# Early fusion block with routed experts: the shared expert of five pairs stands in its own turn instead of in a block behind the main loop

## What is computed

```python
def _L0_ffn_ref(x, gate_w, w1, w3, w2, sw1, sw3, sw2):
    xf = x.reshape(-1, d)
    scores = jax.nn.sigmoid(xf @ gate_w.T)
    top_scores, top_idx = jax.lax.top_k(scores, K)
    ...
    h = jax.nn.silu(einsum('ecd,edh->ech', buf, w1)) * einsum('ecd,edh->ech', buf, w3)
    y = jnp.einsum('ech,ehd->ecd', h, w2)
    ...
    shared = jax.nn.silu(xf @ sw1) * (xf @ sw3) @ sw2
    return (shared + routed).reshape(bs, slen, d)
...
h = jnp.concatenate([tokens(x), txt], axis=1)
h = h + attn(layernorm(h))
h = h + ffn(layernorm(h))
```

## Time and profile before

| | us |
|---|---|
| runs of the kernel before | 1791.42, 1799.02, 1825.51 |
| median | 1799.02 |
| span of the profiled execution | 1823.6 |
| the one run that can hold that span | 1825.51 |
| PE busy (share of the span) | 1534.0 (84%) |
| DVE busy | 1421.6 (78%) |
| ACT busy | 1256.5 (69%) |
| POOL busy | 1226.0 (67%) |

### The profile page before, as it was taken

The page is one execution under the profiler, slowest core; times in us unless marked ns, Lnnn a source line. Parts: engine busy times, 40 slices in busy tenths (PEclk is TensorE's granted clock), DMA queues, the critical chain, the costliest instruction groups (busy, mean ns, idle before and its releaser), DMA issues.

```text
span 1823.6 us, 30829 instructions
## 1 busy us (share of the span) xinstructions
PE 1534.0 (84%) x9237; PEld 1158.6 (64%) x9237; DVE 1421.6 (78%) x5705; ACT 1256.5 (69%) x2195; POOL 1226.0 (67%) x973
## 2 busy tenths in 40 slices
PE   2888998999899999888989898999889975676672
PEld 1566776777676767656767666677667764554552
DVE  3477997999797988777888888889888975587661
ACT  2897997988788878777878787889878851111110
POOL 1025776777676767666667676777667767488887
PEclk9899999999999999999999999999999998899886
DMA  9965666666666666556555655566656221476653
GB/s 182 229 138 120 138 139 125 123 121 124 102 117 100 117 101 106 96 103 103 95 101 104 108 102 102 101 111 105 103 103 103 63 59 40 96 116 109 98 88 35
DMA packets 267117, 197.21 MB, mean 108 GB/s; under 512 B 65464, under 2 KB 246437, under 8 KB 266953
## 3 DMA queue, kind: packets, MB, share of 16 engines
q1 hardware_dynamic: 210120, 174.84, 50.2%
q0 software_dynamic: 51200, 17.87, 8.4%
q10 hardware_dynamic: 5633, 2.56, 0.7%
HBM read 86.24 MB, written 85.39 MB: 94 GB/s over the span
## 4 chain that ended last, share of the span: by engine, by line
PE 40%; ACT 22%; issue 11%; POOL 9%; another core or an unknown queue 8%; DVE 7%; DMA 3%; SPq 0%; ACTq 0%; POOLq 0%; DVEq 0%
POOL out_rows L639 6%; PE bank L919 5%; PE bank L999 5%; ACT img L656 5%; ACT xh L739 4%; PE bank L1087 3%; PE bank L982 3%; POOL slot_rows L605 3%; PE bank L946 2%; PE bank L1018 2%; PE bank L1078 2%; ACT xs L726 2%; ACT kq L793 2%; ACT kq L792 2%
## 5 line engine op out<-in xcount | busy, mean ns | idle before, releaser
L605 POOL DMA_INDIRECT slot_rows<-xs,slot x768 | 874.1, 1138 | 284.5 <-issue 247.3
L656 ACT ACTIVATE img<-img 84x980 f32<-84x980 f32 x190 | 339.6, 1788 | 14.8 <-DMA img<-in_x 7.2
L591 POOL TENSOR_TENSOR rs<-ve,neg_half 128x12 f32<-128x12 f32 (+1 forms) x66 | 150.3, 2277 | 234.4 <-DVE ve L1342 232.8
L919 PE MATMUL bank<-img,w_tok 126*128 126x392 f32 (+1 forms) x640 | 228.7, 505 | 27.9 <-DMA img<-img 23.3
L639 POOL DMA_INDIRECT out_rows<-img,etok x128 | 198.7, 1552 | 64.0 <-issue 35.0
L919 PEld LDWEIGHTS bank<-img,w_tok 126*128 126x128 f32 (+1 forms) x640 | 124.0, 195 | 113.3 <-issue 23.3
L982 PEld LDWEIGHTS bank<-pos_a,v 128*128 128x128 f32 x768 | 145.4, 198 | 54.0 <-issue 10.8
L982 PE MATMUL bank<-pos_a,v 128*128 128x325 f32 (+2 forms) x768 | 163.8, 351 | 6.1 <-issue 3.8
L726 ACT ACTIVATE xs<-h,nb,rs 128x128 f32<-128x128 f32 x384 | 154.0, 481 | 3.0 <-DVE nb L1348 3.0
L739 ACT ACTIVATE xh<-h,nb,rs 128x128 f32<-128x128 f32 x384 | 154.0, 480 | 1.3 <-DVE nb L1348 1.3
L1499 DVE TENSOR_TENSOR h<-bank,hbo 128x768 f32<-128x768 f32 x64 | 61.1, 955 | 114.6 <-remote 103.3
(11 more groups left out here) (217 smaller groups left out, 3697.1 us busy)
## 6 DMA issues: line engine op xcount, KB each, us to landing
img<-in_x SPq DMA_DIRECT2D x384, 150.1 KB
img<-img SPq DMA_DIRECT2D x254, 160.8 KB
img<-img SPq DMA_DIRECT2D x128, 128.6 KB
out_rows<-fin SPq DMA_DIRECT2D x128, 128.0 KB
slot_rows<-xs,slot POOLq DMA_INDIRECT x768
slot_rows<-init_rows SPq DMA_DIRECT2D x16, 540.0 KB, 9.1
img<-slot_rows SPq DMA_DIRECT2D x32, 270.0 KB
h<-in_txt SPq DMA_DIRECT2D x64, 128.0 KB
```

The lines of the kernel that those rows point to most:

```text
L591: g.tensor_tensor(out=rs[:, q.u, half:], in0=ve[:, q.u, half:], in1=neg_half[:, half:], op=ALU.pow).then_inc(S["p_rs"], 1)
L605: g.indirect_dma_start(out=slots_d, out_offset=bass.IndirectOffsetOnAxis(ap=slot[0:nt, q.x, r, part:part + 1], axis=0), in_=xs[0:nt, q.x, ...
L656: a.activation(cols[:, b0:b0 + nb, :], raw[:, q.u, :].rearrange("p (t b) -> p b t", b=P)[:, b0:b0 + nb, :], ACT.Copy)\
L919: ins = mm(bank[:, 5, 0:2 * PATCHES], w_tok[r, m, :], xk[r, k.u, :, m, :], start=(m == 0), stop=(m == SHIFT - 1))
```

## The change

Every pair's shared expert is computed in its own turn. `LATER`, `later`, `rows_of`, `columns_of`, `load_later`, `store_later`, `later_hidden`, `later_out`, `later_product` and `later_sum` go, with their calls, eight semaphores and the buffers `x2_l` and `rows_l`. PE's, POOL's and DVE's waits for the block's semaphores go too. The core of the diff:

```diff
-LATER = tuple(range(8, PAIRS, 11))[0:5]
...
-        x2_l = sb("x2_l", [D, len(LATER), 2, L])
-        rows_l = sb("rows_l", [128, len(LATER) - 1, 2 * NT, D])
...
-            def load_later():
-
-                sp.wait_ge(s_init, 16 * (SLOTS // 1024 + 1))
-                for i, c in enumerate(LATER):
-                    sp.wait_ge(s_store[c % 2], (c // 2 + 1) * 16 * NT)
...
-                    for x, (t0, _) in enumerate(TILES):
-                        sp.dma_start(f[:, x], o[t0:t0 + TILE]).then_inc(l_rows, 16)
...
-                if k.c == PAIRS - 1:
-                    load_later()
...
-            pool.wait_ge(l_store, 16 * NT * len(LATER))
...
-                a.activation(columns_of(z)[:, :, :], bank[:, 1:3, 0:L], ACT.Copy).then_inc(S["a_x2t"], 1)
+                a.activation(x2_t[:, :, :], bank[:, 1:3, 0:L], ACT.Copy).then_inc(S["a_x2t"], 1)
...
-                if later(z):
-                    a.activation(sl[:, 0, 0:TILE], bank[:, 0, 0:TILE], ACT.Silu).then_inc(S["a_sl"], 1)
-                else:
-                    a.activation(sl[:, :, :], bank[:, 0:2, 0:L], ACT.Silu).then_inc(S["a_sl"], 1)
+                a.activation(sl[:, :, :], bank[:, 0:2, 0:L], ACT.Silu).then_inc(S["a_sl"], 1)
...
-            for i in range(len(LATER)):
-                act.wait_ge(l_f1, i + 1)
-                if i == 0:
-                    act.wait_ge(S["v_fin"], PAIRS)
-                else:
-                    act.wait_ge(l_su, i)
-                a.activation(sl[:, :, :], bank[:, 1:3, 0:L], ACT.Silu).then_inc(l_sl, 1)
-                if i > 1:
-                    store_later(i - 2)
...
-                if later(w):
-                    tr(bank[:, 4, 0:TILE], ident, ident).then_inc(S["pe_o"], 1)
-                    return
...
-                if later(z):
-                    tr(bank[:, 4, 0:TILE], ident, ident).then_inc(S["pe_f3b"], 1)
-                else:
-                    mm(bank[:, 4, 0:L], sw3[:, :], x2_t[:, 1, :], start=True, stop=True).then_inc(S["pe_f3b"], 1)
+                mm(bank[:, 4, 0:L], sw3[:, :], x2_t[:, 1, :], start=True, stop=True).then_inc(S["pe_f3b"], 1)
...
-                if not later(z):
-                    mm(bank[:, 1, 0:L], sw1[:, :], x2_t[:, 1, :], start=True, stop=True)
+                mm(bank[:, 1, 0:L], sw1[:, :], x2_t[:, 1, :], start=True, stop=True)
...
-            def later_hidden(i):
...
-                for s in range(2):
-                    ins = mm(bank[:, 1 + s, 0:L], sw1[:, :], x2_l[:, i, s, :], start=True, stop=True)
-                ins.then_inc(l_f1, 1)
-                if i:
-                    pe.wait_ge(l_su, i)
-                for s in range(2):
-                    ins = mm(bank[:, 3 + s, 0:L], sw3[:, :], x2_l[:, i, s, :], start=True, stop=True)
-                ins.then_inc(l_f3, 1)
...
-            def later_out(i):
...
-            later_hidden(0)
-            for i in range(1, len(LATER)):
-                later_hidden(i)
-                later_out(i - 1)
-            later_out(len(LATER) - 1)
-            pe.wait_ge(l_fin, len(LATER))
...
-                if later(w):
-                    vv.tensor_copy(fin[:, w.u], h2[:, w.u]).then_inc(S["v_fin"], 1)
-                    return
...
-                if not later(z):
-                    TT(su[:, :, :], sl[:, :, :], bank[:, 3:5, 0:L], ALU.mult)
+                TT(su[:, :, :], sl[:, :, :], bank[:, 3:5, 0:L], ALU.mult)
...
-            later_product(0)
-            dve.wait_ge(l_rows, 16 * NT * len(LATER))
-            for i in range(1, len(LATER)):
-                later_product(i)
-                later_sum(i - 1)
-            later_sum(len(LATER) - 1)
```

More of the change, by code:

```diff
@@ L132, in uses @@
         return self.c // of + 1
-LATER = tuple(range(8, PAIRS, 11))[0:5]
-def later(pair):
-    return pair.c in LATER
 def first(pair):
@@ L1024, in shared_3b @@
                 wait(pe, S["a_g"], z, -2)
-                if later(z):
-                    tr(bank[:, 4, 0:TILE], ident, ident).then_inc(S["pe_f3b"], 1)
-                else:
-                    mm(bank[:, 4, 0:L], sw3[:, :], x2_t[:, 1, :], start=True, stop=True).then_inc(S["pe_f3b"], 1)
+                mm(bank[:, 4, 0:L], sw3[:, :], x2_t[:, 1, :], start=True, stop=True).then_inc(S["pe_f3b"], 1)
             def shared_1a(z):
-                if later(z):
-                    tr(bank[:, 0, 0:TILE], ident, ident).then_inc(S["pe_f1a"], 1)
-                else:
-                    mm(bank[:, 0, 0:L], sw1[:, :], x2_t[:, 0, :], start=True, stop=True).then_inc(S["pe_f1a"], 1)
+                mm(bank[:, 0, 0:L], sw1[:, :], x2_t[:, 0, :], start=True, stop=True).then_inc(S["pe_f1a"], 1)
             def logits(z):
@@ L1040, in logits @@
                 for s in range(2):
-                    ins = mm(bank[E * s:E * s + E, 2, 0:L], gate_t[:, :], columns_of(z)[:, s, :], start=True, stop=True)
+                    ins = mm(bank[E * s:E * s + E, 2, 0:L], gate_t[:, :], x2_t[:, s, :], start=True, stop=True)
                 ins.then_inc(S["pe_lgt"], 1)
@@ L1046, in shared_1b @@
                 wait(pe, S["v_h2"], z, -1)
[L1047 to L1048 removed]
+                mm(bank[:, 1, 0:L], sw1[:, :], x2_t[:, 1, :], start=True, stop=True)
             def shared_3a(z):
[L1052 to L1053 removed]
+                mm(bank[:, 3, 0:L], sw3[:, :], x2_t[:, 0, :], start=True, stop=True)
             def transpose_1(k):
@@ L1140, in _ @@
             steps(body, 0, 4)
-            def later_hidden(i):
-                if i == 0:
-                    pe.wait_ge(S["a_lgt"], PAIRS)
-                    pe.wait_ge(S["v_fin"], PAIRS)
-                else:
-                    pe.wait_ge(l_sl, i)
-                for s in range(2):
-                    ins = mm(bank[:, 1 + s, 0:L], sw1[:, :], x2_l[:, i, s, :], start=True, stop=True)
-                ins.then_inc(l_f1, 1)
-                if i:
-                    pe.wait_ge(l_su, i)
-                for s in range(2):
-                    ins = mm(bank[:, 3 + s, 0:L], sw3[:, :], x2_l[:, i, s, :], start=True, stop=True)
-                ins.then_inc(l_f3, 1)
-            def later_out(i):
-                pe.wait_ge(l_su, i + 1)
-                if i == 0:
-                    pe.wait_ge(S["a_lg"], PAIRS)
-                else:
-                    pe.wait_ge(l_fin, i)
-                for s in range(2):
-                    for x, (t0, _) in enumerate(TILES):
-                        ins = mm(bank[:, 6 + s, x * D:(x + 1) * D], su[:, s, t0:t0 + TILE], sw2[:, :], start=True, stop=True)
-                ins.then_inc(l_o, 1)
-            later_hidden(0)
-            for i in range(1, len(LATER)):
-                later_hidden(i)
-                later_out(i - 1)
-            later_out(len(LATER) - 1)
-            pe.wait_ge(l_fin, len(LATER))
             def turn(q):
@@ L1618, in _ @@
             steps(body, 0, 4)
-            def later_product(i):
-                dve.wait_ge(l_f3, i + 1)
-                dve.wait_ge(l_sl, i + 1)
-                if i == 0:
-                    dve.wait_ge(S["pe_o"], PAIRS)
-                else:
-                    dve.wait_ge(l_o, i)
-                TT(su[:, :, :], sl[:, :, :], bank[:, 3:5, 0:L], ALU.mult).then_inc(l_su, 1)
-            def later_sum(i):
-                dve.wait_ge(l_o, i + 1)
-                r = rows_of(i).rearrange("p (s t) d -> p s (t d)", s=2)
-                TT(r, bank[:, 6:8, 0:NT * D], r, ALU.add).then_inc(l_fin, 1)
-            later_product(0)
-            dve.wait_ge(l_rows, 16 * NT * len(LATER))
-            for i in range(1, len(LATER)):
-                later_product(i)
-                later_sum(i - 1)
-            later_sum(len(LATER) - 1)
             def prepare(q):
```

14 lines of the change are left out of this document (removed).

## The result

The changed kernel takes 1744.27 us (median of 4 runs, 1739.89 to 1745.25), the kernel before 1799.74 us beside it (4 runs, 1791.42 to 1825.51): ratio 0.9707, 95% interval 0.9658 to 0.9755. That is faster by 2.9%, where the prediction said 1802 us, a range of 1779 to 1825 and "same" with 0.89. The time, the range and the direction are wrong. The profiled execution of the changed kernel took 1743.62 us with a span of 1741.8 us; the one of the kernel before took 1825.51 us, the longest of its four and 26 us over their median.

The account below looks back on a forecast made before the run. The loop was taken as bound by PE, DVE close behind, plus 2.7 us stall a turn, the experts by POOL. The median 1799.0 + 3 for full turns, 0 for the block and the rest, gave 1802 us, range 1779 to 1825.

Parts of the forecast that it names:

- Term 1: Main loop: computing the five light turns in full adds 0.6 us each, +3 us, with ends -2.5 and +13.1.
- case C: Main loop: PE bounds every quick turn, so each filled turn pays PE's full 2.62 us: +13.1, 1812; chance 0.15.
- Rival D: Main loop: late signals depend on where packets break in a turn; 1763 or less, or 1835 or more; chance 0.13.
- Term 2: Behind the loop: in the profiled execution the block held up the experts; removal gives -7.4 us, ends -9.6 and 0.
- what is late next: Behind the loop: without the block PE idles some 28 us and starts at its lower clock; up to 2.2 us return.
- Term 3: Behind the loop: in a usual execution the block lies wholly beside POOL's scatters, so its removal gives 0.
- Case B: Behind the loop: the block is on the path in the usual run too: 1795 us; chance 0.27.
- Term 4: Loads and stores around the loop's end, POOL's wait, eight semaphores, SBUF of two tensors: cost and gain 0.

Follow-up runs that it names:

- f1: Exact copy of the kernel before, on a chip with signals in time: 1664.66 us, ratio 1.0001 to the kernel before.
- c4: The changed kernel with the five light turns back and no block, leaving out five pairs' shared expert: 1662.96 us, ratio 1.0003 to the kernel before.
- d4: The kernel before with all turns full and the block kept, its sums added times zero, on a late-signal chip: 1765.09 us, ratio 0.9835.
- e1: The kernel before with 128 fulfilled waits ahead of PE's first transposes: 1829.42 us, ratio 0.9890; its sibling with 64 waits: 1823.13 us, 0.9882.
- e3: The kernel before with 33 fulfilled waits on PE in each of the five light turns: 1829.26 us, ratio 0.9919.
- e4: The kernel before with all turns full and the block kept, its sums added times zero: 1811.67 us, ratio 0.9811.
- f4: The changed kernel with 128 fulfilled waits ahead of PE's first transposes: 1669.48 us, ratio 1.0031 to the kernel before.
- c1: The changed kernel itself on another chip, signals in time: 1668.33 us against 1663.08 for the kernel before, ratio 1.0032.
- f2: The changed kernel with five light turns and no block, leaving out five pairs' shared expert: 1662.76 us, ratio 0.9989 to the kernel before.
- g2: The changed kernel with five light turns and no block, leaving out five pairs' shared expert, run once more: 1662.81 us, ratio 0.9996 to the kernel before.
- d1: The changed kernel again, on a late-signal chip: 1751.67 us against 1791.23 for the kernel before, ratio 0.9759.
- c2: The changed kernel with the block's two buffers allocated but unused: 1669.16 us, ratio 1.0036 to the kernel before.
- c3: The changed kernel with eight semaphores allocated but unused: 1668.08 us, ratio 1.0039 to the kernel before.
- third batch: Runs on a late-signal chip, the changed kernel among them: 1751.67 us against 1791.23 us for the kernel before.
- d2: The changed kernel with twelve more 4-byte transfers per turn on SyncE's queue: 1782.66 us, 31 us over the changed kernel.
- d3: The kernel before with twelve more 4-byte transfers per turn on SyncE's queue: 1828.32 us, ratio 1.0183.

## Why the prediction was wrong

**Term 1, five turns become full (+3 us).** With signals in time it is a matter of size: I took 0.6 us a turn, and it is 1.13 (f1), 5.6 us in all; the changed kernel against c4, which differs in these turns alone, measured 5.4. The reason given against case C (a light turn's path through DVE keeps it long) was half right: the light turn is DVE's, 0.8 us over DVE's busy time, but the full turn is PE's, so the price lies between the two engines' shares, 1.05 and 2.62. With signals late the term failed in sign: with the five turns full the time fell by 26 us (the kernel before to d4), where +3 was forecast. In the first comparison's traces the gain lies mostly in other turns (36 of them 1.3 us shorter each, the five 1.6). The failing sentence is "Nothing else of a turn moves", together with "These waits are in full and light turns alike": I priced a turn by its own stalls and held the stalls of all others fixed.

**Rival D** had the place and the size: the loop's mean turn moved by 1.3 us in the traces where 0.5 was its mark (by some 0.8, if the 26 us that the trace before is too long are all in its 64 turns), and the time came out under its 1763. It had a chance of 0.13, of which I gave the faster side 0.04. Its mechanism isn't borne out. Moving the boundary left the late signals where they were (e1 to e3: 78.0 to 91.5 us of PE's gaps). Those kernels did win 0.8 to 1.2%; exact copies won nothing, but ran only where signals come in time. So about 1% may belong to any shift of the program, and with it more than half of the 1.65%. That is open. So is whether light turns as such make signals later: on one late chip the time fell by 26 us with full turns, on the other e4's loop was as long as those of e1 to e3, and PE's gaps of the same program are 78.5 us there and 34.1 here (d4). What a chip does to the late signals is larger than what the five turns do. The rule of the Trainium skill weighed in the prediction ("Runtime: NRT & Kernel Launch", "Instruction fetch mechanics": fetching the next block is mostly hidden) agrees with the runs where signals are in time: f4's shift changed nothing, 1.0031 against c1's 1.0032.

**Term 2, the block in the profiled execution (-7.4 us)** was right in kind and 1.4 us short: from the last turn to the first add it was -8.8 us. The step "what is late next" held: first rows 3.04 us after the fetch (1489.31 - 1486.27), first add 13.3 us behind the last scatter (14.7 said), 7.9 us behind the turn of rows (8.9 said).

**Term 3, the block is hidden in a usual execution (0)** is right where signals are in time (f1's rows; c4, f2 and g2, which lack it, at 1.0003, 0.9989 and 0.9996) and wrong where they are late: 13.4 us from d4 to d1. The step that failed is "I hold it more likely than not that the 10.9 us one in the block is among those missing": I took this wait for a rare event. d4's profile has waits of 9.40 and 11.03 us at the same line, and each of the six other late traces with the block has one or two too: on such chips the block waits like this as a rule. The list of waits had hinted at it, with 39 late signals at one line of the loop. Case B, which had the block on the path in the usual run, was right on this point there; it had 0.27.

**Term 4** (0): c2 and c3 bear it out for buffers and semaphores where signals are in time.

**The sum.** Where signals are late, 26.1 us for the turns and 13.4 for the block make the 39.6 us between the medians of the third batch; the forecast had +3 and 0. On a chip with signals in time the steps give 1663.1 + 3 = 1666 and the measurement is 1668.3, well within 2%. The chance of "same" would have been right there. The range failed because it took the 2.7 us of stall in each turn as given, although the prediction itself called them unexplained. An unexplained 12% of a loop is a spread of its own, in both directions.

## What to carry to other kernels

A stall that the profile can't put down to a producer ("remote", an engine idle beside work that was done) isn't part of the cost of a turn; it is a second quantity, which a small edit or another chip can move by more than the edit is worth. Look at the quickest turns for what the work costs (20.0 us here, and 20.28 measured without late signals), and put the rest into the range. Where signals are late, the number of transfers is a cost beside their bytes (31 us for 840 of 4 bytes). Take the trace of a run near the median: here the one before was 26 us over it. And before a win of 3% is explained by the program, run both kernels on a second chip.

## What the hardware showed that I had not expected

- The kernel before took 1791 to 1840 us in three comparisons and 1663 us in three others, on other chips. In the two profiles of it (its own and f1) DVE, ACT and POOL are busy alike to 9 us, the transfers of q1 take the same time to 3 us an engine, and the granted clock is 0.956 and 0.968; PE's records are 56 us longer in sum on the slower chip (1534.0 and 1477.9). On the slower chips signals are late; the change is worth -2.4 to -2.9% there and +0.3% on the others.
- How many changes of a semaphore the trace holds goes with it: 19,719 before and 19,688 after on the first chip, 19,469 to 20,116 in the third batch, with or without the added transfers of d2 and d3, against 37,184 in c1 and 37,543 in f1. Between 300 and 1300 us that is 9.9 to 10.6 per us on the late chips and 24.0 on the others. Records are missing there, and with them many a releaser, so more waits are put down to "remote".
- The lateness begins where the records begin to be missing. Up to 110 us each of the twenty traces holds 1924 to 2051 changes, and the first two turns, from one addition into `h2` to the next, are alike (20.2 to 21.7 us, then 23.9) on all chips. Then the scatters start (at 123 to 126 us in the four traces looked up). The third turn is 20.3 us in all ten traces with signals in time, with 397 to 498 changes in it, and 22.3 to 26.7 us in the ten others, with 183 to 223 changes.
- That signals and records back up on one path of limited rate fits these numbers, but it is argued, and the count alone doesn't carry it: d2 adds 5% of changes and 1.8% of time. The 31 us could also come from the transfers' other traffic, and whether the recording itself takes part isn't told apart.
- Twelve transfers of 4 bytes per turn cost 31 us over the loop's 70 bodies, 0.44 us each, where signals are late. Their cost where signals are in time wasn't measured.
